# RWKV-7 block with an int8 feed-forward on one core: value and old-state products as one 128-row stage

## The chip, the cores and the metric

The kernel runs on one core of one Trainium2 chip. The metric is the device time of one execution in microseconds (us), the median of several runs; lower is better.

## What is computed

The input `x` is 2 sequences of 4096 tokens with 512 channels. A layer norm is followed by an RWKV-7 time mix, whose result is added to `x`; a second layer norm is followed by a feed-forward layer with int8 weights and activations quantised per token, whose result is added as well. The reference, cut to what matters:

```python
mix = x + xx * time_maa_x                       # xx: the token before, minus this one
lo  = einsum(tanh(mix @ maa_w1.T), maa_w2)      # four groups
xrg, xwa, xk, xv = x + xx * (lo + time_maa)
r, k, v = xrg @ Wr.T, xk @ Wk.T, xv @ Wv.T
g = tanh(xrg @ gate_w1.T) @ gate_w2
w = -softplus(-(time_decay + tanh(xwa @ decay_w1.T) @ decay_w2)) - 0.5
a, ma, mk = three sigmoid gates of low rank;  kk = normalised(k + low rank)
k = (k * ma + k * a * (1 - ma)) * exp(w * mk);  b = -kk * a
# per head (16 heads of 32 channels), token after token, w = exp(-exp(w)):
sa = s @ kk
s  = s * w + outer(sa, b) + outer(v, k)
y  = s @ r
y  = group_norm(y) * ln_w + ln_b + (r * k * time_faaaa).sum() * v
x  = x + (y * g) @ Wo.T
x  = x + int8_matmul(layernorm(x), weight_q) * scales + bias
```

The recurrence is computed in chunks of 32 tokens: inside a chunk the steps become a triangular system, and the old state enters as a matrix product.

## The kernel before

**Tiles.** The work goes in 64 tiles (NT) of 64 tokens of both sequences, so 128 tokens. A tile has 2 chunks (NC) for each of 2 sequences and 4 blocks of 128 channels: G = 16 groups of 32 tokens, each holding 4 heads on the 128 partitions (a head is a quadrant of 32 partitions, a pair of heads 64). GS = 8 groups belong to one chunk number `c`; chunk 1 needs the state that chunk 0 leaves.

**Order.** Each engine has an instruction stream of its own, written out by hand in `tile_step(i)`, with semaphores between engines. In step `i` the mixing stage (`mix`) works on tile j = i+1, the projections and gates (`project`) on tile i, the chunked recurrence (`solve`) on m = i-1, and the group norm, output projection and feed-forward (`finish`) on n = i-2. So four tiles are in work at a time, and every engine runs through the stages interleaved.

**The recurrence of one tile.** TensorE (PE) computes scores of removal directions and of keys against the pair of keys and queries in `aq` (`scores_b`, `scores_k`, L1186), three powers of the triangular matrix (`power`, L1208), then `half_inverse` (L1216) and `inverse` (L1224). Then for each chunk c, into one bank (`bank_b` for c = 0, `bank_a` for c = 1):

- `from_values` (L1236): per pair of heads, values `vT2` against the masked key scores and keys `km`, 64 rows contracted, 64 output rows, 96 columns; 8 groups by 2 pairs, so 16 matmuls.
- `from_state` (L1243): the same shape, the decayed old state `s_old2` against `aq` and an identity, added to the same bank; again 16 matmuls.
- `solve_step` (L1252), then `from_solutions` (L1262); VectorE (DVE) takes the right-hand sides out (`right_hand_sides`, L896), and takes the new state out (`update_state`, L900).

A float32 matmul shows as two records in the trace, so 16 matmuls are a row with x32. For a pair of heads, operands have two column halves, one of which is zero where the other head sits (`by_parity` on ScalarE (ACT), with `parity`). `decayed_state` multiplies the state by the chunk's decay `plast`: for c = 0 on GpSimd (POOL), for c = 1 on DVE (both under helper lines L396 and L744).

**The end of a step on DVE.** After `mixed_inputs` on PE (L1122), DVE makes the four mixed inputs from PSUM (`xm_wa`, `xm_k`, `xm_v`, `xm_rg`, L779), POOL adds `xT` to each (L399), and PE's `keys(i+1)` (L1069, `xm_k,w_k`) waits for the last of them, since it writes the bank `xm_rg` is read from. `undecayed` (`bt` L819, `kt` L822) makes the scaled removal vectors and keys. `quantised` on PE (L1281) waits for `xm_wa`, whose bank it overwrites.

**Queues.** All loads and stores of data are issued by SyncE (SP): per tile two loads of `xin` (L284), two stores (L296), two loads of `xres` (L291), each 64 rows of 2 KB. ScalarE switches its function tables where the next function isn't in the loaded set; only once in a step, before `key_decay`, is a set named (`exp_tables`, L643).

## Time and profile before

| | before |
|---|---|
| median of 3 runs | 3234.86 us (3229.97 to 3236.03) |
| span of the profiled execution | 3230.6 us |
| instructions | 182735 |
| PE busy | 3026.2 us, 94% |
| DVE busy | 2659.6 us, 82% |
| ACT busy | 1987.8 us, 62% |
| POOL busy | 1252.0 us, 39% |

The profiled execution's span runs from its first to its last instruction; it has no run time of its own in the list, and its span stands 4.3 us under the median of the runs. Busy time of an engine is the union of its instructions. PEld is the loading of weights into TensorE, which overlaps matmuls. The chain of waits follows the work back from the last instruction to what released it, and "issue" in it is time in which an engine waited for nothing that the profile shows.

### The profile page before, as it was taken

The numbers are of one execution on the slowest core, as the hardware profiler recorded it, in microseconds if no ns is written. First come the engines' busy times: TensorE is split into PE (matmuls) and PEld (weight loads), VectorE is DVE, ScalarE is ACT, GpSimd is POOL, SyncE is SP. The second block draws the span as 40 slices with busy tenths as digits, with TensorE's granted clock in tenths as the row PEclk, the third lists the DMA queues.
The fourth block names the chain that finished last, engine by engine and source line by source line (L and its number), as shares of the span: only waits on it lengthen the run. The fifth ranks groups of instructions, "written<-read, shape, count | busy, mean of one in ns | idle before, by whom it ended". The sixth has DMA issues, their size and how long they took to land.

```text
span 3230.6 us, 182735 instructions
## 1 busy us (share of the span) xinstructions
PE 3026.2 (94%) x84224; PEld 2676.0 (83%) x84224; DVE 2659.6 (82%) x5443; ACT 1987.8 (62%) x3519; POOL 1252.0 (39%) x1161
## 2 busy tenths in 40 slices
PE   5899999999999999999999999999999999999996
PEld 5888888888888888888888888888888888888884
DVE  4687888888888888887888888888888888888885
ACT  3575665665765756756666657567566566566563
POOL 4234334334344344343343343433433433434332
PEclk9999999999999999999999999999999999999998
DMA  3000000000000000000000000000000000000000
GB/s 119 10 23 15 22 20 16 23 20 17 23 20 17 23 20 17 23 20 17 20 18 22 20 17 23 20 17 23 20 17 23 18 18 20 18 22 20 17 17 19
DMA packets 39380, 70.47 MB, mean 22 GB/s; under 512 B 9812, under 2 KB 10836, under 8 KB 38616
## 3 DMA queue, kind: packets, MB, share of 16 engines
q1 hardware_dynamic: 38616, 58.77, 6.7%
q8 instruction: 664, 10.88, 1.4%
q14 instruction: 100, 0.82, 0.1%
HBM read 41.97 MB, written 16.78 MB: 18 GB/s over the span
## 4 chain that ended last, share of the span: by engine, by line
PE 93%; issue 5%; DVE 1%; SPq 1%; ACT 1%; DMA 0%; POOL 0%; POOLq 0%; ACTq 0%; DVEq 0%
PE bank L1069 30%; PE bank_a L1208 12%; PE bank L1272 8%; PE bank_a L1186 4%; PE bank L1076 4%; PE bank_b L1186 4%; PE bank_b L1243 3%; PE bank_b L1236 3%; PE bank_a L1236 3%; PE bank_a L1243 3%; PE bank_a L1216 2%; PE bank_a L1224 2%; PE bank_b L1262 2%; PE bank L1151 2%; PE bank_a L1262 2%
## 5 line engine op out<-in xcount | busy, mean ns | idle before, releaser
L504 ACT ACT_TABLE_LOAD x383 | 491.4, 1283 | 19.3 <-DVE shift L761 12.5
L1069 PE MATMUL bank<-xm_rg,w_r 128*128 128x128 f32 x2048 | 285.4, 282 | 3.5 <-issue 2.7
L1272 PE MATMUL bank<-w_o,yc 128*128 128x512 f32 x512 | 270.8, 630 | 11.1 <-DVE yc L744 9.3
L1208 PE MATMUL bank_a<-pw,w_ffn_int 32*32 32x64 f32 x16384 | 262.0, 215 | 20.1 <-issue 14.9
L1069 PEld LDWEIGHTS bank<-xm_rg,w_r 128*128 128x128 f32 x2048 | 248.9, 191 | 27.9 <-issue 16.9
L1208 PEld LDWEIGHTS bank_a<-pw,w_ffn_int 32*32 32x32 f32 x16384 | 237.4, 105 | 39.4 <-issue 19.0
L1069 PEld LDWEIGHTS bank<-xm_k,w_k 128*128 128x128 f32 x2048 | 241.4, 194 | 12.4 <-issue 3.3
L1069 PE MATMUL bank<-xm_v,w_v 128*128 128x128 f32 x2048 | 249.9, 275 | 1.7 <-DVE kk L744 1.7
L1069 PE MATMUL bank<-xm_k,w_k 128*128 128x128 f32 x2048 | 242.0, 277 | 3.2 <-issue 3.0
L1069 PEld LDWEIGHTS bank<-xm_v,w_v 128*128 128x128 f32 x2048 | 239.2, 192 | 1.8 <-issue 1.8
L504 ACT ACTIVATE u<-bank_b,parity 128x256 f32<-128x256 f32 x128 | 53.7, 470 | 290.8 <-PE bank_b L1252 290.8
L870 DVE STREAM_TRANSPOSE w_ffn_int<-bank_a 128x512 f32<-128x512 f32 x192 | 137.4, 716 | 94.7 <-ACT pw L504 94.4
L399 POOL TENSOR_TENSOR yc<-yc,rkv 128x512 f32<-128x512 f32 x64 | 82.0, 1281 | 327.3 <-ACT yc L504 327.3
L504 ACT ACTIVATE u<-bank_a,parity 128x256 f32<-128x256 f32 x128 | 53.7, 470 | 242.2 <-PE bank_a L1252 242.2
L399 POOL TENSOR_TENSOR xm_wa<-xm_wa,xT 128x512 f32<-128x512 f32 x64 | 75.3, 1177 | 327.9 <-DVE xm_wa L779 327.9
L396 POOL TENSOR_TENSOR kept<-ga,gma 128x512 f32<-128x512 f32 x64 | 81.6, 1274 | 287.1 <-ACT ga L504 287.1
L396 POOL TENSOR_TENSOR kkp<-kk,pinv 128x512 f32<-128x512 f32 x64 | 75.3, 1176 | 288.5 <-DVE kk L744 288.5
L396 POOL TENSOR_TENSOR kmod<-kraw,pinv 128x512 f32<-128x512 f32 x64 | 77.6, 1213 | 258.8 <-ACT pinv L504 258.8
L1208 PE MATMUL bank_a<-first,w_ffn_int 32*32 32x64 f32 x8192 | 134.9, 215 | 26.2 <-issue 25.3
L399 POOL TENSOR_TENSOR o_sb<-o_sb,x2b 128x512 f32<-128x512 f32 x64 | 81.7, 1276 | 200.5 <-DVE o_sb L968 200.5
L396 POOL TENSOR_TENSOR qkT<-qkT,faaaa_T 128x512 f32<-128x512 f32 x64 | 81.5, 1273 | 166.5 <-DVE qkT L914 166.5
L744 DVE TENSOR_TENSOR first<-bank_a,mask_b 128x1024 f32<-128x1024 f32 x64 | 78.4, 1225 | 81.6 <-PE bank_a L1186 81.6
(204 smaller groups left out, 8579.9 us busy)
## 6 DMA issues: line engine op xcount, KB each, us to landing
xin<-in_x SPq DMA_DIRECT2D x128, 128.0 KB, 2.7
xres<-in_x SPq DMA_DIRECT2D x128, 128.0 KB
out<-o_sb SPq DMA_DIRECT2D x128, 128.0 KB, 2.5
w_ffn_int<-in_weight_q SPq DMA_DIRECT2D x1, 2048.0 KB, 9.7
w_k<-in_Wk SPq DMA_DIRECT2D x1, 1024.0 KB
w_r<-in_Wr SPq DMA_DIRECT2D x1, 1024.0 KB
w_v<-in_Wv SPq DMA_DIRECT2D x1, 1024.0 KB
w_o<-in_Wo SPq DMA_DIRECT2D x1, 1024.0 KB, 14.9
```

Source lines behind the costliest of these rows:

```text
L396: return nc.gpsimd.tensor_tensor(out_, in0, in1, ALU.mult)
L399: return nc.gpsimd.tensor_tensor(out_, in0, in1, ALU.add)
L504: return nc.scalar.activation(out_, in_, func, **kw)
L870: V.transpose(pt, pairs(bank_a)[:, :, 0, :]).then_inc(v_ptT, 1)
L1069: ins = mm(bank[:, o * n:(o + 1) * n], weights[:, k, o * P:(o + 1) * P], x[:, k].rearrange("p b t -> p (b t)"), start=(k == 0), stop=(k == ...
L1076: ins = mm(bank[:, o * TOK:(o + 1) * TOK], weights[:, o * P:(o + 1) * P], hidden[:], start=True, stop=True)
L1186: ins = mm(bank[q, 64 * n:64 * n + 64], both(keys_[q, g]), both(aq[q, g, 0:2]), start=True, stop=True)
L1208: ins = mm(bank_a[q, 64 * n:64 * n + 64], pt[q, g, :], source[q, g, 0:2].rearrange("p j t -> p (j t)"), start=True, stop=True)
L1236: mm(bank[q, 4 * CHUNK * j:4 * CHUNK * j + 3 * CHUNK], both(vT2[q, g]), km[q, g].rearrange("p j t -> p (j t)"), start=(j % 4 == 0), stop=F ...
L1243: ins = mm(bank[q, 4 * CHUNK * j:4 * CHUNK * j + 3 * CHUNK], both(s_old2[q, j]), aq[q, g].rearrange("p j t -> p (j t)"), start=False, stop ...
L1262: ins = mm(bank[q, 4 * CHUNK * j + CHUNK:4 * CHUNK * j + 3 * CHUNK], both(u2[q, j]), first[q, g, 2:4].rearrange("p j t -> p (j t)"), start ...
L1272: ins = mm(fb[0][:], yc[:, k * TOK:(k + 1) * TOK], w_o[:, k, :], start=(k == 0), stop=(k == KB - 1))
```

## The change

The products from values and from the old state, two matmuls of 64 contracted rows for each pair of heads and group, become one of 128 contracted rows. `stacked` holds, for a pair, the values of both heads in its lower 64 partitions and the state of both heads in its upper 64; `streamed` holds masked key scores and keys in the lower 64 and the decayed keys, queries and decay diagonal in the upper 64. Since engines don't move a pair of heads by 64 partitions here, four DMAs per tile on SP's queue, each of 64 partitions by 6 KB (384 KB), carry them: two from `aq_state` (`move_queries`) and two from `km` (`move_keys`). GpSimd makes `aq_state` (`state_queries`: one instruction of 1024 and one of 512 elements per partition) in the place of its `decayed_state`; both `decayed_state` and `enter` (`plast`) are gone. `update_state` is four transposes of 32 partitions instead of one of 128, written straight into `stacked`; `value_pairs` is four ScalarE instructions of 64 partitions instead of two of 128. Some buffers are laid on others, with a few waits added for that. The order of all engines' streams is new, and ScalarE's sets are named, four switches in a step.

```diff
+        stacked = sb("stacked", [P, 2, G, 2, HS])
+        streamed = sb("streamed", [P, 3, 2, G, CHUNK])
...
+            def move_queries(m):
+                sp.wait_ge(g_aqs, count(m, 1, 1))
+                sp.wait_ge(p_rhs, count(m, NC, 0))
+                for pair in range(2):
+                    sp.dma_start(streamed[P // 2:, :, pair], aq_state[two_heads(pair)]).then_inc(queries_moved, 16)
+
+            def move_keys(m):
+                sp.wait_ge(v_km, count(m, 1, 1))
+                sp.wait_ge(v_klT, count(m, 1, 1))
+                sp.wait_ge(p_rhs, count(m, NC, 0))
+                for pair in range(2):
+                    sp.dma_start(streamed[:P // 2, :, pair], km[two_heads(pair)]).then_inc(keys_moved, 16)
...
+            def state_queries(m):
+                pool.wait_ge(v_q, count(m, 1, 1))
+                pool.wait_ge(queries_moved, count(m, 32, 0))
+                whole = pinv[:, :, 0:1]
+                mul(aq_state[:, 0:2], aq[:], whole.unsqueeze(1).to_broadcast([P, 2, G, CHUNK]))
+                mul(aq_state[:, 2], ident32[:].unsqueeze(1).to_broadcast([P, G, HS]),
+                    whole.to_broadcast([P, G, HS])).then_inc(g_aqs, 1)
...
             def value_pairs(m):
                 act.wait_ge(v_vT, count(m, 1, 1))
-                act.wait_ge(p_s, count(m, NC, 0))
-                by_parity(vT2, vT[:]).then_inc(a_vT2, 1)
+                act.wait_ge(p_rhs, count(m, NC, 0))
+                for pair in range(2):
+                    for h in range(2):
+                        ins = run(stacked[:P // 2, pair, :, h, :], vT[two_heads(pair)], ACT.Identity,
+                                  scale=parity[two_heads(pair), h:h + 1])
+                ins.then_inc(a_vT2, 1)
...
             def update_state(m, c):
                 dve.wait_ge(p_s, count(m, NC, c + 1))
-                V.transpose(state[(c + 1) % 2][:], step_part(c, NEW)).then_inc(v_state, 1)
-
-            def decayed_state(m):
-                dve.wait_ge(v_state, count(m, NC, 2))
...
+                for h in range(QH):
+                    to = stacked[quad(2 + h % 2), h // 2, :, h % 2, :].rearrange("p (g c) t -> p g c t", c=NC)
+                    ins = V.transpose(to[:, :, 1 - c, :], step_part(c, NEW)[quad(h)])
+                ins.then_inc(v_state, 1)
...
-            def from_values(m, c):
+            def from_values_and_state(m, c):
                 bank = step_bank(c)
                 if c == 0:
                     pe.wait_ge(a_vT2, count(m, 1, 1))
-                    pe.wait_ge(v_klT, count(m, 1, 1))
-                    pe.wait_ge(v_km, count(m, 1, 1))
+                    pe.wait_ge(keys_moved, count(m, 32, 32))
+                    pe.wait_ge(queries_moved, count(m, 32, 32))
                 if c == 1:
                     pe.wait_ge(v_t, count(m, 1, 1))
-                for j, g, q in step_pairs(c):
-                    mm(bank[q, 4 * CHUNK * j:4 * CHUNK * j + 3 * CHUNK], both(vT2[q, g]),
-                       km[q, g].rearrange("p j t -> p (j t)"), start=(j % 4 == 0), stop=False, skip_group_check=True)
-
-            def from_state(m, c):
...
-                pe.wait_ge(sold, count(m, NC, c + 1))
-                for j, g, q in step_pairs(c):
-                    ins = mm(bank[q, 4 * CHUNK * j:4 * CHUNK * j + 3 * CHUNK], both(s_old2[q, j]),
-                             aq[q, g].rearrange("p j t -> p (j t)"), start=False, stop=False, skip_group_check=True)
+                pe.wait_ge(v_state, count(m, NC, c + 1))
+                for j in range(GS):
+                    g = j * NC + c
+                    for pair in range(2):
+                        ins = mm(bank[two_heads(pair), 4 * CHUNK * j:4 * CHUNK * j + 3 * CHUNK],
+                                 both(stacked[:, pair, g]), streamed[:, :, pair, g],
+                                 start=(j % 4 == 0), stop=False, skip_group_check=True)
                 ins.then_inc(p_rhs, 1)
...
+            EXP_LN, SIGMOID_TANH = "natural_log_exp_and_others", "sigmoid_and_others"
...
+            def tables(functions):
+                nc.scalar.preload_act_table_set(functions)
```

What moves in a full step is shown at two places. First PE, from the half inverse to the second chunk's products. In the rows `tx`, `rhs_sb` is the solve step, `first,u` is `from_solutions`, `w_o,yc` the output projection, `w_maa` the low-rank matmul of the mixing. Before:

```order
L1216 MATMUL bank_a<-pw,w_ffn_int 32x32 x64
L1272 MATMUL bank<-w_o,yc 128x512 x2
L1069 MATMUL bank<-mix,w_maa 128x128 x4
L1224 MATMUL bank_a<-pw,w_ffn_int 32x16 x64
L1243 MATMUL bank_b<-aq,s_old 64x96 x16
L1272 MATMUL bank<-w_o,yc 128x512
L1252 MATMUL bank_b<-rhs_sb,tx 32x32 x32
L1069 MATMUL bank<-xm_rg,w_gate 128x128 x4
L1262 MATMUL bank_b<-first,u 64x64 x16
L1076 MATMUL bank<-hid_g,w_gate 128x128 x4
L1236 MATMUL bank_a<-km,vT 64x96 x16
L1243 MATMUL bank_a<-aq,s_old 64x96 x16
```

and now:

```order
L1248 MATMUL bank_a<-pw,w_ffn_int 32x32 x64
L1271 MATMUL bank_b<-streamed,stacked 64x96 x16
L1135 MATMUL bank<-ident,xn 128x128 x4
L1256 MATMUL bank_a<-pw,w_ffn_int 32x16 x64
L1301 MATMUL bank<-w_o,yc 128x512
L1101 MATMUL bank<-xm_v,w_v 128x128 x4
L1281 MATMUL bank_b<-rhs_sb,tx 32x32 x32
L1301 MATMUL bank<-w_o,yc 128x512
L1101 MATMUL bank<-xm_rg,w_gate 128x128 x4
L1291 MATMUL bank_b<-first,u 64x64 x16
L1101 MATMUL bank<-xn,w_maa 128x128 x4
L1108 MATMUL bank<-hid_g,w_gate 128x128 x4
```

The joined product of chunk 0 (L1271) stands right behind the half inverse; before, the values' part (L1236, not in this piece) stood further ahead, behind the third power, and the state's part behind the inverse. The joined product of chunk 1 follows the last row directly, and the low-rank matmul has moved in ahead of it.

Second DVE, at the end of a step, with the four mixed inputs, `bt` and `kt` of `undecayed`, and the state. Before:

```order
L779 SCALAR_TENSOR_TENSOR xm_wa<-bank,maa,xx 128x128 x4
L779 SCALAR_TENSOR_TENSOR xm_k<-bank,maa,xx 128x128 x4
L779 SCALAR_TENSOR_TENSOR xm_v<-bank,maa,xx 128x128 x4
L919 STREAM_TRANSPOSE rkv<-qkT 128x512
L779 SCALAR_TENSOR_TENSOR xm_rg<-bank,maa,xx 128x128 x4
L819 SCALAR_TENSOR_TENSOR bt<-ga,kkp 128x512
L822 SCALAR_TENSOR_TENSOR kt<-kept,kmod 128x512
L900 STREAM_TRANSPOSE state<-bank_a 128x256
```

and now:

```order
L815 SCALAR_TENSOR_TENSOR xm_wa<-bank,maa,xx 128x128 x4
L815 SCALAR_TENSOR_TENSOR xm_k<-bank,maa,xx 128x128 x4
L815 SCALAR_TENSOR_TENSOR xm_v<-bank,maa,xx 128x128 x4
L855 SCALAR_TENSOR_TENSOR bt<-ga,kkp 128x512
L859 SCALAR_TENSOR_TENSOR kt<-kept,kmod 128x512
L815 SCALAR_TENSOR_TENSOR xm_rg<-bank,maa,xx 128x128 x4
L938 STREAM_TRANSPOSE stacked<-bank_a 32x8x32 x4
```

`bt` and `kt` now stand between the third and the fourth mixed input, where the transpose `rkv` stood, and the one transpose of the state is four. The two products `aq` have left this place for one in the middle of the step.

## Rows read from the trace of the kernel before

**Rows 1.** The page: span, busy time by engine, chain by engine.
```profile
span 3230.6 us, 182735 instructions
...
PE 3026.2 (94%) x84224; PEld 2676.0 (83%) x84224; DVE 2659.6 (82%) x5443; ACT 1987.8 (62%) x3519; POOL 1252.0 (39%) x1161
...
PE 93%; issue 5%; DVE 1%; SPq 1%; ACT 1%; DMA 0%; POOL 0%; POOLq 0%; ACTq 0%; DVEq 0%
```
**Rows 2.** Busy time in one stretch: length, then PE, PEld, DVE, ACT, POOL.
```profile
170.46:3119.00 2948.54, 2820.81 (x79002) 2498.17 (x79004) 2488.17 (x5100) 1865.39 (x3303) 1159.72 (x1021) 1.00 0.07 20
```
**Rows 3.** SP's timeline: store of the first full step and of the 60th behind it.
```profile
171.86 1.15 SPq L296 DMA_DIRECT2D out<-o_sb  x2
...
3119.18 1.49 SPq L296 DMA_DIRECT2D out<-o_sb  x2
```
**Rows 4.** The chain of waits in two steps: start us, us, what.
```profile
1508.39 1.92 PE bank_a L1208 x128
...
1517.56 1.47 PE bank_b L1236 x32
...
1522.58 1.91 PE bank L1272 x4
...
1526.58 1.47 PE bank_b L1243 x32
...
1533.12 1.47 PE bank_a L1236 x32
1534.59 1.34 PE bank_a L1243 x32
...
1586.17 1.10 PE bank L1122 x32
...
1587.96 0.68 issue
...
1593.00 3.57 PE bank L1069 x32
```
**Rows 5.** VectorE's timeline at the end of a step.
```profile
1587.41 1.12 DVE L779 SCALAR_TENSOR_TENSOR xm_wa<-bank,maa,xx 128x128 f32<-128x128 f32 x4
...
1590.52 0.70 DVE L919 STREAM_TRANSPOSE rkv<-qkT 128x512 f32<-128x512 f32 x1
1591.14 1.09 DVE L779 SCALAR_TENSOR_TENSOR xm_rg<-bank,maa,xx 128x128 f32<-128x128 f32 x4
```
**Rows 6.** VectorE's groups by shape: count, busy us and mean ns, idle before.
```profile
L822 DVE SCALAR_TENSOR_TENSOR kt<-kept,kmod 128x512 f32<-128x512 f32 x64 | 106.0, 1657 | 0.0
L744 DVE TENSOR_TENSOR s_old<-state,plast 128x512 f32<-128x512 f32 x64 | 84.8, 1325 | 2.2
...
L819 DVE SCALAR_TENSOR_TENSOR bt<-ga,kkp 128x512 f32<-128x512 f32 x64 | 44.1, 689 | 0.0
...
L900 DVE STREAM_TRANSPOSE state<-bank_b 128x256 f32<-128x256 f32 x64 | 28.8, 450 | 72.5 <-PE bank_b L1262 72.5
```
**Rows 7.** ScalarE's groups by shape.
```profile
L504 ACT ACT_TABLE_LOAD x383 | 491.4, 1283 | 19.3 <-DVE shift L761 12.5
...
L504 ACT ACTIVATE vT<-vT,parity 128x512 f32<-128x512 f32 x128 | 84.6, 710 | 0.0
...
L643 ACT ACT_TABLE_LOAD x64 | 82.1, 1283 | 1.1
```
**Rows 8.** GpSimd's groups by shape.
```profile
L399 POOL TENSOR_TENSOR xm_rg<-xm_rg,xT 128x512 f32<-128x512 f32 x64 | 99.3, 1552 | 14.9 <-DVE xm_rg L779 14.9
...
L396 POOL TENSOR_TENSOR w_ffn_int<-aq,kt 128x512 f32<-128x512 f32 x64 | 81.7, 1276 | 0.0
```
**Rows 9.** DMAs of the page: KB each, median us to landing; then L284's spread.
```profile
xin<-in_x SPq DMA_DIRECT2D x128, 128.0 KB, 2.7
...
w_ffn_int<-in_weight_q SPq DMA_DIRECT2D x1, 2048.0 KB, 9.7
...
DMA to landing us min/median/max: 2.4/2.7/11.8
```

More of the change, by code:

```diff
@@ L145, in rwkv_ffn_kernel @@
         u2 = sb("u2", [P, GS, 2, HS])
-        state = [sb(f"state{n}", [P, GS, HS]) for n in range(2)]
-        s_old2 = sb("s_old2", [P, GS, 2, HS])
         gate = sb("gate", [P, W])
@@ L453, in residual_bias @@
             def residual_bias(n):
+                pool.wait_ge(v_x2, count(n, 1, 1))
                 add(x2b[:], xres[:], ffn_bias[:]).then_inc(g_x2b, 1)
@@ L550, in squares @@
                 act.wait_ge(v_sqT, count(i, 1, 0))
+                if i >= 2:
+                    act.wait_ge(v_ysqT, count(i - 2, 1, 1))
                 run(sq[:], kk[:], ACT.Square).then_inc(a_sq, 1)
@@ L684, in tile_step @@
                 if project:
+                    tables(SIGMOID_TANH)
+                    ma_gate(i)
+                    a_gate(i)
+                if solve:
+                    power(m, 0)
+                if project:
+                    squares(i)
                     decay_gate(i)
                 if solve:
+                    value_pairs(m)
                     power(m, 1)
@@ L849, in token_major_keys @@
                 dve.wait_ge(v_k, count(m, 1, 1))
-                V.transpose(km[:, :, 2, :], kt[:]).then_inc(v_klT, 1)
+                dve.wait_ge(p_sk, count(m, 1, 1))
+                dve.wait_ge(keys_moved, count(m, 32, 0))
+                V.transpose(km[:, 2], kt[:]).then_inc(v_klT, 1)
                 V.transpose(first[:, :, 3, :], bt[:]).then_inc(v_blT, 1)
@@ L1186, in scores @@
                     ins = mm(bank[q, 64 * n:64 * n + 64], both(keys_[q, g]),
-                             both(aq[q, g, 0:2]), start=True, stop=True)
+                             aq[q, :, g], start=True, stop=True)
                 return ins
```

257 lines of the change are left out of this document (124 added, 133 removed).

## The prediction

> **What bounds the kernel now.** I read the page first. TensorE is busy for 94% of the span, the other engines for 82% and less, and the chain of waits is 93% TensorE [rows 1]. So time is gained where TensorE does less or waits less, and nowhere else until another engine catches up with it. Then the size of one step. From the store of the first full step to the 60th behind it are 3119.18 - 171.86 = 2947.3 us [rows 3], so a step takes 49.1 us. In that stretch TensorE is busy 2820.8 us of 2948.5 [rows 2]: 47.0 us of work and 2.1 us of idleness per step. VectorE works 2488.2 / 60 = 41.5 us of it and idles 7.7 us. The granted clock there is 1.00, so full speed, 2.4 GHz. Of TensorE's idleness 0.68 us is the wait ahead of `quantised` [rows 4], which ends with `xm_wa` on VectorE: that one ran from 1587.41 for 1.12 us, to 1588.53 [rows 5]. The other 1.4 us or so the profile calls "issue". It cannot be taken away by this change except by chance.
>
> **TensorE's products.** The four stages that become two take 1.47 + 1.47 + 1.47 + 1.34 = 5.75 us per step [rows 4], each of 16 matmuls of 64 rows by 64 output rows and 96 columns. Two new stages hold 16 matmuls each, of 128 rows by 64 output rows and 96 columns. The question on which all hangs is whether two of them, which share all rows of the array and use different output halves, run side by side.
> - If not, a matmul costs what a full one costs per column. The `keys` row has 16 matmuls of 128 columns in 3.57 us [rows 4], 0.223 us each; for 96 columns that is 0.167, and 2.68 us per stage. The dearest reading leaves the columns out: 3.57 us.
> - If they do, a stage costs as the old pair stage, 1.47 us, at the least 1.34.
> - No row shows this shape. The nearest says: the matmuls of `mixed_inputs` use different rows and share all output columns, and 16 of them with 128 columns take 1.10 us [rows 4], 0.069 each against 0.223, so three at a time. Sharing one side of the array doesn't stop matmuls from running together there. The old pair stages, which share neither side, need 0.092 us each against 0.167 for a lone matmul, so 1.8 at a time. I take 1.47 us per stage: 5.75 - 2.94 = 2.8 us less per step. The other ends are a gain of 3.1 (1.34), of 0.4 (2.68) and a loss of 1.4 us (3.57).
>
> The Trainium skill, "TensorE: Matmul & The Clock Gate", Part 3 (packing small matmuls), gives 2.38 times for three tiles that differ only in columns. As an estimate from that page, two such tiles would run at 1.6 times, a stage would take 1.69 us and the gain would be 2.4 us instead of 2.8. No row here shows it.
>
> Whether the loading of weights stays hidden matters too, since all new matmuls use the same rows. The `keys` matmuls do so as well and cost 0.223 / 128 = 1.74 ns per column; those of the output projection, which load a fourth as often per column, cost 1.91 / 1024 = 1.87 ns [rows 4]. So loading is hidden there. The same part of the page says that weights load beside running matmuls only when the row groups differ, with the background buffer as the exception. By the rule without the exception the second pair would wait for the first, which is rival 3; the two rows side with the exception.
>
> **VectorE.** `s_old` of chunk 1 goes, 1.33 us [rows 6], and the small `plast`, which I leave out of the sum. `update_state` becomes 8 transposes instead of 2. One of 128x256 takes 0.45 us [rows 6]; the new ones have the same 256 elements per partition on a quarter of the partitions. Bounds: the full 0.45 each, or a quarter, 0.11. I take 0.45, since each instruction walks its elements per partition: +6 x 0.45 = 2.7, in sum +1.4 us, 42.9 us per step (with 0.11: -1.3). This lies beside TensorE's work as long as VectorE keeps up. On the path from chunk 0 to chunk 1 nothing is lost: four transposes, 1.8 us, stand where a transpose and `s_old` took 0.45 + 1.33 us.
>
> **VectorE's end of a step.** This is the one new wait that I count. `keys` needs all of `xm_rg`. Before, `mixed_inputs` ended on TensorE at 1586.17 + 1.10 = 1587.27, `xm_rg` on VectorE at 1591.14 + 1.09 = 1592.23 [rows 4, 5], 4.96 us later, and `keys` began at 1593.00, 5.73 us later: TensorE had other work until then. Now `rkv` (0.70) leaves this stretch and `bt` (0.69) and `kt` (1.66) enter it [rows 5, 6]: 4.96 + 1.65 = 6.6 us. TensorE's own work in between is the same, 5.73 us with its 0.68 of waiting. So `keys` waits 0.9 us more. `kt` takes 1.66 us against 0.69 for `bt`, the same kind of instruction, while GpSimd's `xm_rg` sum beside it takes 1.55 us [rows 6, 8]; both then read two operands from SBUF. Now GpSimd's `xm_v` stands beside it, so I keep the dear price. Bounds: 0 (VectorE is ahead there) to 0.9. I take 0.9, the row's.
>
> **ScalarE, GpSimd.** Table loads go from (383 + 64) / 64 = 7 to 4 per step, 3 x 1.28 = 3.8 us less [rows 7]. `value_pairs` goes from 2 to 4 instructions at no more than 0.71 us each [rows 7], +1.4. ScalarE is 62% busy; both stay hidden behind TensorE, and I cost them at nothing. GpSimd's `state_queries` has 1536 elements per partition, three times the 1.28 us of a product of 512 [rows 8], 3.8 us, against 1.1 for its old `s_old`. It has the room (39% busy), and what it delays is first the DMA below. If that cover went, 2.7 us per step would be the price.
>
> **The DMAs.** Four of 384 KB per step on SP's queue. 128 KB land after 2.7 us and 2048 KB after 9.7 us [rows 9], so 3.6 us per MB beyond 2.3: a pair, 768 KB, lands after 5.0 us. The keys' pair is the late one: it waits for `token_major_keys`, which now stands behind the second power on VectorE. From there to the joined product TensorE has five projection blocks (0.89 each, 4.5 us), a power (1.92) and two output blocks (1.91), 8.3 us, and the half inverse, which I leave as margin [rows 4]. ScalarE's copy and three VectorE instructions before the DMA, at 0.7 each [rows 6], take 2.8. That leaves 5.5 us for 5.0: just hidden. SP itself then waits with `load_x`, a store and `load_residual` behind these moves; each of these is needed a step or half a step later, so they cost nothing. Two further places of the new order hold, as far as these rows tell. `shift_mix` now follows `decayed` on VectorE, and the low-rank matmul has moved behind chunk 0's solutions to allow for it. The joined product of chunk 1 waits for the state, with `w_maa` and the output gate as TensorE's work in between: 1.8 us against the 1.8 of the transposes.
>
> **Sum.** -2.8 + 0.9 = -1.9 us per step, over 64 steps -122 us. From the span of 3230.6 us that is 3108; the median of the runs stands 4.3 us above the span, so 3112, rounded to **3110 us**. A measurement of this kernel can tell about 0.2%, 6 us, from no change.
>
> **The rivals.**
> 1. *TensorE's waits go too.* The new order avoids the wait at `keys`, and half of the 1.4 us of "issue" is not met. Another 1.6 us per step, 3010 us. For it: a wait on one of seven placed stages is easily moved. Against it: "issue" has no releaser that an order could serve. 15%.
> 2. *VectorE becomes the bound.* At 47.2 us per step its idleness must shrink from 7.7 to 4.3 us. If half of these 3.4 us stays, a step takes 48.9 us and the time is 3222 us; if a quarter, 3165. Against it: most of its waits are for TensorE and shrink with it. 15%, at 3165 to 3225.
> 3. *The columns don't run side by side* (slower). A stage takes 2.68 us: -0.4 + 0.9 = +0.5 us per step, 3235 + 32 = 3267 us. The point from which it decides is a stage of 2.43 us: there 5.75 - 4.86 = 0.9 is eaten by the wait at `keys`. For it: no matmul in this trace shares its rows with another at the same time. Against it: `mixed_inputs` shares the other side. 16%.
> 4. *The moves come late* (slower). If a pair needs the 9.7 us of the row of 2048 KB, it is 4.2 us late, TensorE stands before the joined product and the step is 2.3 us longer than before: 3380 us. It decides from a landing of 7.4 us on. For it: L284's longest was 11.8 us [rows 9]. Against it: its median was 2.7. 7%.
>
> The forecast itself has 47%, at 3060 to 3160 us.
>
> **How the numbers follow.** Faster by over 0.2%: the forecast, rival 1, most of rival 2 (13%) and a little of rival 3 with no wait at `keys` (2%): 0.77. Within 0.2%: the edges of rivals 2 and 3, 0.06. Slower: 0.17. The range must reach from the dearer half of rival 1 through rival 3 up to its price: 3010 to 3267 us leaves out half of rival 1, rival 4 and some of rival 3, near 2 in 10. The likeliest case alone is 3060 to 3160.
>
> **What would show it.** Right: the stage of 128 rows (x32 in the chain) takes about 1.5 us, a step from store to store about 47.2 us, a wait for `xm_rg` stands before `keys`, and the pairs land within 5.5 us. Wrong: a stage of 2.7 us (rival 3), VectorE over 93% busy with TensorE waiting for powers or right-hand sides (rival 2), or a wait before the joined product that ends with a DMA (rival 4). Then the sum falls at that term.

## The result, and the profile after

The changed kernel takes **3366.68 us** (median of 4 runs, 3364.70 to 3367.22) against 3235.45 us (4 runs, 3229.97 to 3238.58) for the kernel before: the ratio is 1.0407, with a 95% interval of 1.0392 to 1.0421. It is slower by 131 us, where 3110 us and a gain had been forecast. (Times of one kernel differ from chip to chip: on the chips of the experiments below the kernel before takes 3217 to 3225 us. So the ratios, each taken on one chip, say what a change is worth; microseconds of two traces are compared for where they go.) The page of the changed kernel: span, busy time by engine, DMA queue of the data, chain by engine.

```profile
span 3365.5 us, 175696 instructions
...
PE 2931.0 (87%) x80128; PEld 2550.6 (76%) x80128; DVE 2887.9 (86%) x5699; ACT 1831.5 (54%) x3457; POOL 1444.6 (43%) x1224
...
q1 hardware_dynamic: 91864, 159.45, 19.8%
...
PE 63%; DVE 27%; issue 8%; DMA 1%; POOL 0%; ACT 0%; SPq 0%; POOLq 0%; DVEq 0%; ACTq 0%
```

Beside [rows 1], TensorE works 95 us less and the kernel is 135 us longer in span: its idle time has grown from 204 to 434 us. The chain of waits, 93% TensorE before, now runs through VectorE for 27% of the span. The stores of the first full step and of the 60th behind it, SP's timeline, to set beside [rows 3], and busy time in that stretch, to set beside [rows 2] (length, then PE, PEld, DVE, ACT, POOL, granted clock, DMA share, GB/s):

```profile
171.70 1.17 SPq L297 DMA_DIRECT2D out<-o_sb  x2
...
3248.96 1.15 SPq L297 DMA_DIRECT2D out<-o_sb  x2
```

```profile
171.70:3248.96 3077.26, 2728.08 (x75126) 2376.86 (x75124) 2702.45 (x5341) 1715.14 (x3242) 1338.41 (x1081) 0.99 0.21 49
```

A step takes 3077.26 / 60 = 51.3 us, 2.2 more than before. TensorE works 45.5 us of it (47.0 before) and idles 5.8 (2.1 before). So 1.5 us of work went, not 2.8, and 3.7 us of idleness came. Where it sits is in the view of TensorE's waits of the changed kernel (line and what it waited for: us in total, times, longest):

```profile
PE bank L1101 <- DVE xm_rg L815: 77.4, 62, 2.1
PE bank_a L1240 <- issue: 66.7, 70, 2.1
PE bank_a L1256 <- issue: 65.5, 64, 2.5
PE bank L1310 <- issue: 56.6, 54, 1.1
...
PE bank_a L1248 <- issue: 18.1, 27, 1.6
```

The same view of the kernel before:

```profile
PE bank_a L1208 <- issue: 40.2, 47, 1.6
PE bank L1281 <- issue: 40.0, 59, 0.7
...
PE bank_a L1216 <- issue: 12.5, 15, 1.2
PE bank_a L1224 <- issue: 11.5, 16, 1.1
```

I add up all rows of this view for both kernels. Rows with "issue" sum to 262 us after and 134 before, rows with a named releaser to 158 after and 59 before. With 95 us less work, 128 + 99 - 95 = 132 us, which is the loss but for 3 us of the 135 between the spans. Of the named waits, 77 us are the keys' wait for the queries' input. "Issue" is the larger part, and it isn't one kind. L1310 (L1281 before) are the transposes of the quantised rows; they wait for `xm_wa` in both kernels, as the forecast read it, and have grown by 17 us. Without them "issue" is 205 us against 94, 1.7 us per step more, and that looks different. TensorE's timeline of one step (start us, us, what; in brackets the idle time before):

```profile
1631.56 1.16 PE L1256 MATMUL bank_a<-pw,w_ffn_int 32*32 32x16 f32 x116
1634.43 0.40 PE L1256 MATMUL bank_a<-pw,w_ffn_int 32*32 32x16 f32 x12 [1.71 <-issue]
1634.76 2.08 PE L1301 MATMUL bank<-w_o,yc 128*128 128x512 f32 x2
```

The inverse is 64 matmuls, 128 records. After 116 of them TensorE stands for 1.71 us and then does the last 12. All of the group's semaphores had come before its first matmul, so no engine is waited for. In the gap and behind it the granted clock is the lower one (windows of 2 us, columns as above):

```profile
1633.00:1635.00 2.00, 0.56 (x13) 0.53 (x13) 0.13 (x1) 0.00 (x0) 0.00 (x0) 0.51 0.00 0
1635.00:1637.00 2.00, 2.00 (x4) 0.97 (x5) 2.00 (x4) 0.00 (x0) 0.00 (x0) 0.50 0.03 8
1637.00:1639.00 2.00, 2.00 (x48) 1.78 (x50) 1.23 (x5) 0.42 (x1) 0.00 (x0) 0.50 0.00 0
1639.00:1641.00 2.00, 2.00 (x49) 1.46 (x39) 0.18 (x1) 1.54 (x5) 0.00 (x0) 0.78 0.00 0
1641.00:1643.00 2.00, 2.00 (x41) 1.81 (x40) 1.74 (x6) 1.27 (x1) 0.27 (x1) 1.00 0.03 8
```

0.50 is 1.2 GHz, 1.00 is 2.4 GHz. A block of the output projection (x2) takes 2.08 us there, where two blocks (x4) took 1.91 in [rows 4]. Ahead of this TensorE had stood for 1.14 us, worked 2.2 us and stood for 1.71 us again; the clock is low from within that second stop until shortly before 1640. It isn't so in every step: in the next one the two stops nearest to this place were 0.76 and 1.08 us, and the granted clock stayed at 1.00. Part of the forecast's 2.8 us of work went this way. How much can be estimated: in windows of 2 us over the stretch from the first full step to the 60th behind it, the part of the clock that was not granted, times TensorE's busy time, sums to 42 us in the changed kernel and 5 us in the kernel before, so some 37 us. Single rows are a poor guide to it: the output projection is busy 285.9 us against 270.8 and the values 288.0 against 249.9, but the products `xm_rg,w_r` beside them 257.6 against 285.4.

What ends these stops can be read from the trace's DMA packets. The page counts a queue of instructions; after, then before:

```profile
q8 instruction: 632, 10.35, 1.3%
...
q8 instruction: 664, 10.88, 1.4%
```

A packet there is 16 KB. The changed kernel has 8192 records of TensorE (matmuls and weight loads) fewer and 32 packets fewer, so this queue brings TensorE's instructions, 256 records to a packet. The inverse and the half inverse have 256 records each, and work through them in 1.3 to 1.5 us where nothing holds them; no two packets start closer together than 3.3 us. In the step above there is one packet in 1628:1629 and one in 1631:1632, and none between or behind them up to 1635:

```profile
q8 instruction: 1, 0.02, 6.5%
...
q8 instruction: 1, 0.02, 8.0%
```

They start at 1628.20 and 1631.83, and the two stops end at 1630.50 and 1634.43, 2.3 and 2.6 us later. Over the whole run, of the 227 stops behind "issue" apart from L1310 (205 us), 226 end between 2.0 and 3.1 us after a packet's start; a moment taken at random lies there in 21% of the cases. So these stops read as waits for the next packet of instructions.

### The profile page after: what moved, and what is told of

Read it like the earlier page. It is cut to its first block, busy times and chain, and to the rows that moved or that the text cites. A ratio compares the mean times of both kernels' runs of the same rounds, so it can differ in the third digit from the quotient of the medians.

```text
span 3365.5 us, 175696 instructions
## 1 busy us (share of the span) xinstructions
PE 2931.0 (87%) x80128; PEld 2550.6 (76%) x80128; DVE 2887.9 (86%) x5699; ACT 1831.5 (54%) x3457; POOL 1444.6 (43%) x1224
## 4 chain that ended last, share of the span: by engine, by line
PE 63%; DVE 27%; issue 8%; DMA 1%; POOL 0%; ACT 0%; SPq 0%; POOLq 0%; DVEq 0%; ACTq 0%
PE bank L1101 22%; PE bank_a L1240 11%; PE bank L1301 8%; DVE stacked L938 4%; PE bank_a L1218 3%; PE bank_b L1218 3%; PE bank_b L1271 3%; DVE kt L859 3%; PE bank_a L1256 3%; PE bank_a L1248 2%; DVE x2n L985 2%; PE bank_b L1291 2%; DVE xm_rg L815 2%; DVE xm_k L815 2%; DVE xm_v L815 2%
## 5 line engine op out<-in xcount | busy, mean ns | idle before, releaser
L474 POOL TENSOR_TENSOR rs<-rs,minus_half 128x1 f32<-128x1 f32 x64 | 35.0, 548 | 1168.1 <-DVE rs L981 1168.1
L1101 PE MATMUL bank<-xm_k,w_k 128*128 128x128 f32 x2048 | 246.6, 279 | 79.1 <-DVE xm_rg L815 77.4
L1101 PEld LDWEIGHTS bank<-xm_v,w_v 128*128 128x128 f32 x2048 | 269.6, 204 | 58.8 <-issue 53.1
L1240 PEld LDWEIGHTS bank_a<-pw,w_ffn_int 32*32 32x32 f32 x16384 | 242.9, 106 | 82.9 <-issue 60.4
L1101 PE MATMUL bank<-xm_v,w_v 128*128 128x128 f32 x2048 | 288.0, 291 | 14.2 <-issue 14.1
L1301 PE MATMUL bank<-w_o,yc 128*128 128x512 f32 x512 | 285.9, 663 | 9.3 <-DVE yc L780 9.3
L1101 PE MATMUL bank<-xm_rg,w_r 128*128 128x128 f32 x2048 | 257.6, 279 | 0.8 <-issue 0.7
L526 ACT ACTIVATE pw<-bank_a 128x512 f32<-128x512 f32 x192 | 114.2, 595 | 150.3 <-PE bank_a L1240 146.2
L526 ACT ACTIVATE val<-bank 128x512 f32<-128x512 f32 x64 | 38.2, 597 | 270.7 <-PE bank L1101 270.7
L526 ACT ACTIVATE stacked<-vT,parity 64x512 f32<-64x512 f32 x256 | 169.8, 711 | 0.8
L526 ACT ACTIVATE xT<-bank 128x512 f32<-128x512 f32 x64 | 38.2, 597 | 210.1 <-PE bank L1135 210.1
L1256 PE MATMUL bank_a<-pw,w_ffn_int 32*32 32x16 f32 x8192 | 93.4, 180 | 65.5 <-issue 65.5
L1256 PEld LDWEIGHTS bank_a<-pw,w_ffn_int 32*32 32x32 f32 x8192 | 81.2, 105 | 82.1 <-issue 81.8
```

The source lines that it names most:

```text
L526: return nc.scalar.activation(out_, in_, func, **kw)
L1101: ins = mm(bank[:, o * n:(o + 1) * n], weights[:, k, o * P:(o + 1) * P], x[:, k].rearrange("p b t -> p (b t)"), start=(k == 0), stop=(k == ...
L1240: ins = mm(bank_a[q, 64 * n:64 * n + 64], pt[q, g, :], source[q, g, 0:2].rearrange("p j t -> p (j t)"), start=True, stop=True)
L1256: ins = mm(bank_a[q, HALF * n:HALF * (n + 1)], pt[q, g, :], pw[q, g, 1, HALF:], start=True, stop=True)
L1301: ins = mm(fb[0][:], yc[:, k * TOK:(k + 1) * TOK], w_o[:, k, :], start=(k == 0), stop=(k == KB - 1))
```

## What the engines behind the keys' wait do

VectorE's timeline at the end of the same step, to set beside [rows 5], and GpSimd's up to there:

```profile
1642.80 1.83 DVE L938 STREAM_TRANSPOSE stacked<-bank_b 32x256 f32<-32x256 f32 x4 [0.15 <-PE bank_b L1291]
1644.67 1.17 DVE L985 TENSOR_SCALAR x2n<-xres,mv,rs 128x512 f32<-128x512 f32 x1
...
1651.27 0.96 DVE L855 SCALAR_TENSOR_TENSOR bt<-ga,kkp 128x512 f32<-128x512 f32 x1
1652.15 1.66 DVE L859 SCALAR_TENSOR_TENSOR kt<-kept,kmod 128x512 f32<-128x512 f32 x1
1653.74 1.11 DVE L815 SCALAR_TENSOR_TENSOR xm_rg<-bank,maa,xx 128x128 f32<-128x128 f32 x4
```

```profile
1642.73 0.55 POOL L474 TENSOR_TENSOR rs<-rs,minus_half 128x1 f32<-128x1 f32 x1 [21.31 <-DVE rs L981]
1643.25 1.17 POOL L417 TENSOR_TENSOR kmod<-kraw,pinv 128x512 f32<-128x512 f32 x1
1644.37 1.18 POOL L417 TENSOR_TENSOR kkp<-kk,pinv 128x512 f32<-128x512 f32 x1
1645.51 1.46 POOL L417 TENSOR_TENSOR kmod<-kmod,z 128x512 f32<-128x512 f32 x1
```

From chunk 0's solutions at 1642.80 to the keys at 1655.00 VectorE has no gap that matters: 12.2 us of work in one row, with the four transposes of the state (0.45 us each) and the quantiser ahead of the mixed inputs. GpSimd shows a second thing, which lies in the new order: `norm2_rstd` stands ahead of `undecayed`, so three products whose operands are ready wait 21 us for a rstd (the reciprocal standard deviation) of another tile, and then run beside VectorE's quantiser. `x2n` takes 1.17 us there and took 0.55 before.

## The experiments

Every ratio is to the kernel before on the same chip, with its 95% interval. A per cent is some 32 us, or 0.5 us per step. Step lengths are read from the stores as above. "The stage" is the joined product.

**e1: without the DMAs.**

```diff
-                    move_queries(m)
-                    move_keys(m)
...
+                then(pool.memset(streamed[:], 0.0))
```

> The changed kernel without its four DMAs per step; the joined stage multiplies a buffer that is set to zero once, so the moved keys and queries are left out of the result, and all other work and waits stay. Theory A (the extra 1.5 MB per step slow the fetching of TensorE's instructions): the idle time called issue falls back from about 3.9 to 1.4 us per step, the half-clock stretches mostly go, and the time falls by 120 to 180 us to 3190 to 3250 us. Theory B (the new order packs stages of many small matmuls behind each other, so that fetching falls behind by itself): issue time before L1256 stays near 65 us in sum and the time falls by less than 40 us.

1.0263 [1.0238, 1.0288], a step of 50.3 us. The moves cost 1.0 us per step of the 2.2. The stage doesn't wait for them in a row of the waits, so they do it otherwise: "issue" in all rows sums to 217 us instead of 262. That is 46 us less, between the two theories: too little for theory A, and "issue" before the inverse (56.7 us instead of 65.5) stays about where theory B had it. The edit takes out the waits for the DMAs as well as the DMAs.

**e2: the kernel before, with four such DMAs per step** into a buffer that nothing reads.

> The kernel before with four more DMAs of 384 KB per step on SyncE's queue, copying its keys and queries to a buffer that nobody reads. Theory A: issue time rises from about 1.4 by 1 to 2.5 us per step and the time by 60 to 160 us, to 3295 to 3395 us. Theory B: no more than 20 us, under 3255 us.

1.0111 [1.0088, 1.0134], a step of 49.6 us against 49.1. Traffic alone, with no one waiting for its data, costs 36 us there. It lies between the two expectations, too. The trace is 26 us longer than that of the kernel before: 16 us are "issue" (149 us), 10 us are TensorE's busy time, and the named waits are unchanged.

**e3: `xm_rg` ahead of `bt` and `kt` on VectorE.**

> The changed kernel with undecayed (bt, kt) behind the fourth mixed input on VectorE again. If the wait for xm_rg before keys (77.4 us in sum) is a cost of its own, it goes and the time falls by 60 to 90 us, to 3280 to 3305 us. If it only moves (scores wait for bt2 and kt2, made 2.4 us later, or VectorE's whole chain is the bound), the time changes by less than 25 us.

1.0514 [1.0490, 1.0539]: the keys' wait goes and the scores' wait for `bt` comes (87.6 us at L1218, which waits for ScalarE's pairs of `bt`). That is 10 us more than what it replaced, and waits at the powers grow beside it: the named waits sum to 200 us instead of 158. So it went the second way of the expectation, the wait moves, and costs more than was expected there.

**e4: TensorE's short stages spaced** by output and value blocks.

> The changed kernel with one block of values and one of the output projection put between the half inverse and the joined product, and one of the output projection between the joined product and the inverse, as the order before had it. Theory B: issue time before the inverse (65.5 us in sum) falls to under 20 us and the time by 50 to 100 us, to 3265 to 3315 us. Theory A: the gaps move to other stages and the time changes by less than 25 us.

1.0578 [1.0551, 1.0604]. At the inverse "issue" falls from 65.5 to 6.5 us, and at the half inverse (L1248) it rises from 18.1 to 70.3. "Issue" as a whole hardly changes (256 us instead of 262): the gap belongs to the run of short matmuls, not to one stage. The time rises by 1.7%, which neither theory had; the named waits, 201 us instead of 158, are where it goes, among them 17 us for `stacked`.

**e5: three of the four transposes of the state left out**, so the state is wrong for three heads in four.

> The changed kernel with only the last of the four transposes of update_state for each chunk, so three quarters of the state never reach the stage; VectorE has 2.7 us less per step, 1.35 us of it on the way from chunk 0 to chunk 1. If VectorE's chain sets the step, the time is 80 to 170 us less than the changed kernel's (ratio to before 0.99 to 1.015). If the supply of TensorE's instructions sets it, under 40 us less (ratio over 1.028).

1.0277 [1.0262, 1.0292]. The transposes cost 0.9 us per step of VectorE's row, and the keys' wait stays (77.9 us), since all of VectorE's row moves up with the state. The ratio stands just under the 1.028 from which the supply of instructions alone was to set the time: both have a part.

**e6: the joined stage in the order of the kernel before**, on all engines.

> The joined stage with its DMAs, state_queries and transposes, but in the order of the kernel before on TensorE, ScalarE, VectorE and GpSimd; the joined product stands where from_state stood. If the new order costs the time, this one is at 0.97 to 1.0 of before (products -2.8 us per step, DMAs +0.5, a wait for the state +0.9). If the stage itself costs it, the ratio is 1.02 or more.

1.0694 [1.0675, 1.0713]. TensorE's waits in e6:

```profile
PE bank L1133 <- ACT xn L528: 130.9, 62, 16.1
PE bank_a L1216 <- ACT w_ffn_int L528: 79.6, 51, 2.0
PE bank_a L1238 <- DVE pw L779: 69.1, 59, 2.4
PE bank_a L1269 <- DVE stacked L937: 59.4, 64, 0.9
```

So the new order isn't the loss by itself: the stage as built here is dearer still in the old one, where other engines are late in four places. One is the state's transposes (`stacked`). Two are ScalarE's, and these aren't shown to be the stage's longer way for data (products on GpSimd, a DMA, four transposes): e6 keeps seven table loads per step, has `value_pairs` at four instructions, and keeps the buffers laid on others with the waits added for that. ScalarE is busy 2079 us in it, 1988 before and 1832 in the changed kernel. No run takes these apart. What is bought with the new order shows in the other sum. "Issue" is 137 us in e6, as in the kernel before, and 262 in the changed kernel: the growth came with the order.

**e7: the kernel before without `from_values`**, so values don't enter the outputs. By the rows of the forecast that is 2.94 us per step less for TensorE, and nothing less for the others.

> The kernel before with the matmuls of from_values left out (2.94 us of TensorE per step), its waits kept; the values' part of the result is missing. If TensorE's time counts in full, as the prediction had it, 180 us less than before, ratio 0.944. If what TensorE gains is mostly given back as issue gaps, since those matmuls gave its instruction supply time to catch up, or as waits for VectorE, less than 90 us, ratio over 0.972.

0.9945 [0.9928, 0.9961]: 18 us gained of 188 us taken away. TensorE's waits in e7:

```profile
PE bank_a L1239 <- DVE s_old L744: 59.8, 64, 1.3
PE bank L1103 <- ACT xn L504: 59.6, 47, 14.6
...
PE bank_a L1216 <- issue: 26.4, 19, 1.8
```

Between the two traces TensorE's busy time falls by 154 us, and the named waits grow from 59 to 171. TensorE was busy for 94% before, but the work of other engines stood right behind it: `s_old` and `xn` become the ends that are waited for. This is the run that speaks to the forecast's first sentence. It speaks for these matmuls: half of them stood in TensorE's stream between chunk 0's solutions and the product from the decayed state, so they covered the 60 us for which e7 waits for `s_old`.

**e8: the kernel before with the named function tables** (`tables(...)` at the four places). **e12** is e7 and e8 together.

> The kernel before with ScalarE's table sets named at four places, order as before; four loads per step instead of seven. ScalarE isn't waited for by TensorE in the profile, so no change beyond 10 us, ratio 0.997 to 1.003. If its lateness is hidden in the issue gaps, 20 us or more less.

> The kernel before without the matmuls of from_values and with ScalarE's sets named. Leaving the matmuls out gave 18 us, with waits for ScalarE's xn in the place of TensorE's work; naming the sets alone gave 6. If ScalarE's lateness is what had been covered, both together give clearly more than 24 us: 60 us or more, ratio under 0.981. If the state's way (s_old) and the issue gaps are, no more than 30 us, ratio over 0.99.

0.9983 [0.9968, 0.9997] and 0.9895 [0.9866, 0.9924]. Three loads fewer per step give 5 us where TensorE is full, and some 16 us where TensorE has room (the two intervals together allow 5 to 27). That is neither the 60 us in sum that would make ScalarE's lateness the cover, nor quite over 0.99. e8 is the only one of these kernels that computes everything and is faster than the kernel before, if barely.

**e9: `undecayed` ahead of `norm2_rstd` on GpSimd**, in the changed kernel.

```diff
                 if finish:
                     add_bonus(n)
-                    norm2_rstd(n)
                 if project:
                     undecayed(i)
+                if finish:
+                    norm2_rstd(n)
```

> The changed kernel with GpSimd's undecayed ahead of its norm2_rstd, which waits for VectorE's residual and holds up all that is queued behind it (21 us idle per step in the profile). If that queueing costs time (x2n on VectorE runs 1.17 us beside the late products instead of 0.55), 25 to 45 us less than the changed kernel. If the products only slow other VectorE instructions instead, within 10 us.

1.0282 [1.0244, 1.0320], a step of 50.3 us: 40 us for one moved line. The first instruction of the quantiser is back near its old price, 561 ns against 1170 in the changed kernel and 550 before (VectorE's groups, before and in e9):

```profile
L952 DVE TENSOR_SCALAR x2n<-xres,mv,rs 128x512 f32<-128x512 f32 x64 | 35.2, 550 | 0.7 <-POOL rs L451 0.7
...
L986 DVE TENSOR_SCALAR x2n<-xres,mv,rs 128x512 f32<-128x512 f32 x64 | 35.9, 561 | 2.8 <-POOL rs L474 0.7
```

The transposes of the quantised rows wait 41.9 us as "issue" instead of 56.6, so the quantiser's late start was what had grown there. The keys' wait stays (73.7 us).

**e10: e9 with VectorE's quantiser ahead of the state**, the output projection earlier, `undecayed` behind the state.

> As e9, and the stretch from chunk 0's solutions to keys shortened on VectorE: the output projection is finished before the solve step, the quantiser stands ahead of the state's transposes, bt and kt stand behind them. Theory V (VectorE's tail of the step sets its length, with the issue gaps): the wait for xm_rg goes, a step takes 48.0 to 49.5 us, the ratio to before is 0.975 to 1.01. Theory F (the supply of TensorE's instructions gives back what is gained): issue gaps grow by as much, ratio over 1.025.

1.0627 [1.0594, 1.0659]. The keys' wait is gone; in its place one wait of 2.8 us per step:

```profile
PE bank_a L1272 <- DVE stacked L939: 181.7, 63, 4.7
```

GpSimd's rstd stood behind `kmod * z` now, which waits for ScalarE's exponential, and the quantiser and the state stood behind the rstd. **e11**, e10 with GpSimd writing the queries itself and no DMA for them, kept this wait (181.8 us), made GpSimd later (TensorE's output projection now waits 60 us for `yc`) and came to 1.0833 [1.0795, 1.0871], where less than e10 was expected. It computes everything, so an engine can carry a pair of heads over by 64 partitions itself; here that is dearer than the DMA.

> As e10, but GpSimd writes decayed queries straight into the upper 64 partitions of the streamed operand, four instructions of 64 partitions in the place of two of 128 and two DMAs, so half the moved bytes. From the run without DMAs (46 us less for four) I expect 15 to 30 us less than e10; if GpSimd's longer instructions (3 us more per step) get in the way of VectorE or of the product, as much more.

**e13: e10 with GpSimd's rstd between `kkp` and `kmod * z`. e14: the same without the DMAs.**

> e10 with one move on GpSimd: rstd of the second norm goes between kkp and kmod*z, so that the quantiser no longer waits behind ScalarE's exponential. Theory C (the chain on VectorE before the keys is what holds the step, and e10 only hid it behind the queue on GpSimd): the wait of the state product for stacked falls from 2.8 us per step to under 0.5, the wait for xm_rg stays away, ratio 1.00 to 1.015. Theory D (waits on this kernel change place, the time of a step is not in one chain): the stacked wait falls, but others grow, ratio 1.025 to 1.05.

> e13 without the four DMAs per step (streamed is zeroed once, so the stage of values and old state reads stale zeros in half of its rows). Theory C: 0.012 to 0.016 under e13's ratio, as e1 stood to the changed kernel, so 0.985 to 1.00. Theory D: less than 0.008 under e13.

1.0553 [1.0530, 1.0576] and 1.0415 [1.0390, 1.0441]. e13 refutes theory C and went past theory D, whose range ended at 1.05: the stacked wait hardly falls (162 us), now because the quantiser's chain on VectorE (the residual, five instructions, `x2n` again at 1.48 us) stands ahead of the state. The keys' wait cost 1.2 us per step in e9, this one costs 2.5. That e14 is 0.014 lower was theory C's figure and not theory D's, so the DMAs' cost is one of its own.

**e15: e9 without the DMAs.**

> e9 without the four DMAs per step (streamed zeroed once, the stage reads zeros in half of its rows). If the cost of the DMAs (0.014 of the time before, e1) and of GpSimd's order (0.012, e9) add, the ratio is 1.012 to 1.018; if both lengthen the same operations and are one cost, 1.020 to 1.028.

1.0102 [1.0078, 1.0126], a step of 49.5 us. It is 0.018 under e9, where e1 was 0.014 under the changed kernel: the two costs add, and a little more.

**e16: e9 with `xm_rg` behind `bt`, ahead of `kt` alone. e17: the same without the DMAs.**

```diff
                     undecayed(i)
                 if mix:
                     mixed_inputs(j, XRG, XRG)
+                if project:
+                    undecayed_keys(i)
```

> e9 with one more move on VectorE: the queries' input (xm_rg) comes ahead of kt, behind bt. If the end of the tile's chain on VectorE is what the next keys wait for, the wait for xm_rg (1.2 us per step) goes and nothing takes its place, since kt is wanted 15 us later: ratio 1.028 less 0.02, so 1.005 to 1.015. If time on this kernel only changes place, xm_rg's wait goes and the ratio stays at 1.022 to 1.03.

> e16 without the four DMAs per step (streamed zeroed once, half of the product's rows are zeros). The DMAs cost 0.014 in e1 and 0.018 in e15, so e16's ratio less 0.014 to 0.018; below 1 only if e16 is below 1.015.

1.0119 [1.0080, 1.0158] and 0.9976 [0.9953, 0.9999]; steps of 49.4 and 48.6 us. What e3, e10 and e13 did not get, this does: the keys' wait goes, the waits with a named releaser sum to 74 us (141 in e9, 59 before) and no other named wait takes their place, since `bt` is wanted at once and `kt` late; "issue" rises from 232 to 249 us. Part of the gain is a cheaper `kt`: behind `xm_rg` it no longer runs beside GpSimd's `xm_v` and takes 676 ns, where it took 1649 in e9, 1.0 us per step less on VectorE.

```profile
L862 DVE SCALAR_TENSOR_TENSOR kt<-kept,kmod 128x512 f32<-128x512 f32 x64 | 43.3, 676 | 0.0
```

e16 is the best kernel with the joined stage that computes everything, and still 1.2% slower than the kernel before.

**e18: fewer short matmuls, the same time on TensorE.** In e9, the second round of `power` is replaced, so the inverse isn't the reference's.

```diff
-                for n, g, q in ALL:
+                for n, g, q in ALL if k != 1 else ():
...
+                for h in range(2) if k == 1 else ():
+                    ins = mm(bank_a[:, 512 * h:512 * (h + 1)], w_o[:, h, 0:P], w_o[:, h, :], start=True, stop=True)
```

> e9 with the second of the three rounds of power (64 matmuls of 32 rows and 64 columns, 2.1 us, in the trace 128 records) replaced by two matmuls of 128 rows and 512 columns with w_o, also some 2.1 us by w_o's rows, so the inverse is not computed rightly. Theory E (TensorE runs out of instructions behind many short matmuls): the idle time put down to issue falls from 3.1 to under 2.2 us per step, ratio 1.005 to 1.015. Theory F (the idle time belongs to other things): issue within 0.3 us per step, ratio 1.023 to 1.033.

0.9960 [0.9940, 0.9980], a step of 48.9 us against e9's 50.3. "Issue" sums to 170 us, against 232 in e9: 1.0 us per step less, as theory E had it. Two rows of e18's waits:

```profile
PE bank_a L1259 <- issue: 49.7, 50, 2.5
...
PE bank_a L1241 <- issue: 15.3, 16, 2.2
```

At the powers (L1241) it fell from 65.3 to 15.3 us, at the inverse (L1259) only from 55.2 to 49.7. The two long matmuls, 122 us in all, are also 14 us shorter than the round they replace (half of 272), 0.2 us per step. The two traces add up so: "issue" falls by 63 us and TensorE's busy time by 49 (those 14, some 11 that the same estimate as above puts on the clock, the rest not traced), and the named waits rise by 21 (141 to 162), in sum 91 of the 90 us between the spans. The gain is larger than theory E's range. Taken together: idle time without a releaser inside a group that has all its operands, which follows the run of short matmuls when stages are moved (e4), is half as large in the old order (e6), shrinks when 124 of a step's matmul records and as many weight loads go at nearly equal TensorE time (e18) and somewhat when DMA traffic goes (e1, e15). This fits an engine that gets its instructions slower than it can run short ones, and the packets of the instruction queue show the supply itself: e18 has 570 of them instead of 632, and in e18 as in e1, e6 and the kernel before, all but 1 to 5 of the stops behind "issue" (apart from the quantised rows) end 2.0 to 3.1 us after a packet's start. No run changes the supply alone.

## Why the prediction was wrong, step by step

**Right.**
- *The columns run side by side.* The stage takes 1.54 us for x32 in the timeline, as a stage from values did there before (1.54 at 1583.31), for which the chain's 1.47 had been taken; 2.68 would have been rival 3:

```profile
1644.78 1.54 PE L1271 MATMUL bank_a<-streamed,stacked 128*64 128x96 f32 x32
```

- *The transposes of the state* cost 448 ns each, 0.45 was taken.
- *The keys' wait* was forecast at 0.9 us per step, the upper of its bounds, and is 77.4 / 64 = 1.2. Its mechanism was right. The piece missing is `bt`, at 0.95 instead of 0.69 us.
- *The landing* of a pair was forecast at 5.0 us. The DMAs of the keys' pair have a median of 5.3 (for the queries' the profile has none), and rival 4's wait for the DMA is 0.5 us in the whole run.

```profile
streamed<-w_ffn_int SPq DMA_DIRECT2D x128, 384.0 KB, 5.3
```

**Wrong.** Over 64 steps the sum had -180 us for TensorE's work, +58 us for the keys' wait and nothing for all else. The two traces have -95 us for the work, +99 us for the named waits (77 of them the keys') and +128 us for "issue". So "issue" was put at nothing and is half of the miss, the work that goes is short by 85 us, and the waits by 41. The steps behind these terms:
1. *"So time is gained where TensorE does less or waits less, and nowhere else until another engine catches up with it"*, with -2.8 us per step counted in full. Busy for 94% is not the same as alone on the path. e7 takes 2.94 us per step off the same engine and gains 0.3: other engines' results were due only just in time. The forecast's rival 2 had this as VectorE's business and gave it 15%. It doesn't hold for every saving on TensorE, though: e18 takes 49 us of work and 63 us of "issue" off and gains some 104 (0.032 of the time). And the two waits of e7 are not what the changed kernel lost by: with its new order it waits 2.6 us for `stacked` and 18.4 us for `xn`.
2. *"The other 1.4 us or so the profile calls issue. It cannot be taken away by this change except by chance."* It was treated as fixed, and it nearly doubled: 2.0 us per step more, 1.7 of it apart from the quantised rows' wait. It is the largest term of the miss, and its growth was in no rival; rival 1 had it shrink. What the traces show in its place is the supply of TensorE's instructions: 256 records to a packet, and packets at least 3.3 us apart there. The new order sets the half inverse, the stage, four transposes and the inverse in one row, 148 matmuls of which 144 are short, where before two output blocks and the low-rank matmul stood between the half inverse and the inverse. The order of TensorE shown ahead of the prediction holds this.
3. *The lower clock* was not in the sum at all. Work fell by 1.5 instead of 2.8 us per step; the 1.3 us between are 83 us over the run. In the step shown the output projection and the values stand in a stretch at 0.50. The estimate above puts some 37 of the 83 us on the clock; the others stay open.
4. *"both stay hidden behind TensorE, and I cost them at nothing"*, said of ScalarE, with GpSimd costed at nothing as well ("It has the room"). Counting GpSimd's work was not enough: where `norm2_rstd` stands in its queue holds three products for 21 us and makes VectorE's quantiser dearer beside them. e9 prices that at 40 us.
5. *"just hidden"*, of the DMAs, which were put at nothing. It was right for their landing. They cost 36 to 58 us all the same (e2, e1, e15), 36 by traffic alone.
6. *"This lies beside TensorE's work as long as VectorE keeps up"*, of the state's transposes, and on their way to chunk 1 *"1.8 us against the 1.8 of the transposes"*. They also stand ahead of everything else in VectorE's last 12 us, which is what the next keys wait for; e5 prices three of them at 0.9 us per step, 42 us.

The three settled pieces give the loss back: GpSimd's line (e9, 1.2%), VectorE's end (e16, another 1.6%) and the DMAs (e17, another 1.4%) lead from 1.041 to 0.998. So even with all three gone (and the moved data with them) the change is worth 8 us (0 to 15 by the interval), not the 122 forecast, and 5 of them are what the named table sets give by themselves (e8). What then still stands against it is "issue" at 221 us in e17, 87 more than before.

Open: why a packet of instructions comes no sooner, and how the traffic of the other DMAs lengthens the stops, since without it the packets start no closer together either (3.25 us at the least in e1); what the rest of e18's gain beyond "issue" is; and whether an order exists that keeps e16's waits and sets long matmuls between all short stages. That last kernel wasn't tried.

## What to carry to other kernels

A busy share of 94% says how much an engine works, not that a microsecond taken from it is a microsecond gained: before costing a saving, leave the work out of the kernel before and time that, as e7 did, and look whether it had covered a wait. When an order is changed, read "issue" as a term of its own: count TensorE's records, and where 256 of them take well under 3.3 us for more than one packet in a row, look for stops there. In a queue written by hand, look at each instruction for who stands behind it: one line of GpSimd's, moved down by one place, was worth 40 us.

## What the runs showed of the hardware that had not been expected

- TensorE's instructions come in packets of 16 KB with 256 matmul and weight-load records each (632 packets in the changed kernel, 664 before), which start 3.2 us apart or more in every run. TensorE's stops without a releaser end 2.0 to 3.1 us after such a start, in 226 of 227 cases.
- TensorE stops inside a group of short matmuls whose operands are all there, for up to 2.5 us, and stops less with fewer of them (e18) or less DMA traffic (262 us to 217 in e1).
- With the second of two such stops, 1.14 and 1.71 us, the granted clock fell to 0.50, half of full speed, for some 7 us, and a block of the output projection there took 2.08 us instead of about 1.
- DMA traffic that nobody waits for costs time: 100 MB more over the run, 36 us (e2).
- Work of VectorE on SBUF beside GpSimd's products gets longer: `x2n` 0.55 to 1.17 us, `bt` 0.69 to 0.95 us. With GpSimd's products moved away `x2n` is back at 0.56 (e9), and `kt`, 1.66 us in the kernel before, takes 0.68 (e16).
- A transpose of 32 partitions costs what one of 128 does, 448 against 450 ns, and a copy of ScalarE on 64 partitions 711 against 710 ns for 128: splitting these two by partitions made each part as dear as the whole.
